# The order in which attention takes its sixteen (group, chunk) pairs: two groups mixed, or one group after the other

## The reference

```python
q = _rope(proj(Wq, bq), e); k = _rope(proj(Wk, bk), e); v = proj(Wv, bv)
att = jnp.einsum('bhqd,bhkd->bhqk', q, k) / scale
att = jnp.where(causal[None, None], att, -jnp.inf)
att = jax.nn.softmax(att, axis=-1)
y = jnp.einsum('bhqk,bhkd->bqhd', att, v)   # then the output projection
...
x = x + 0.5 * ffn(layernorm(x))     # ffn: attention, router, top 2 of 8 experts
x = x + attn(layernorm(x))
x = x + 0.5 * ffn(layernorm(x))
```

## Time and profile before

| | us |
|---|---|
| median of 3 runs | 1795.04 |
| lowest and highest | 1793.52, 1797.59 |
| profiled execution | 1790.89 |
| its span, first to last instruction | 1789.1 |

### The profile page before, as it was taken

The page is one execution under the profiler, slowest core; times in us unless marked ns, Lnnn a source line. Parts: engine busy times, 40 slices in busy tenths (PEclk is TensorE's granted clock), DMA queues, the critical chain, the costliest instruction groups (busy, mean ns, idle before and its releaser), DMA issues. The chain is left out here.

```text
span 1789.1 us, 31832 instructions
## 1 busy us (share of the span) xinstructions
PE 1629.0 (91%) x11268; PEld 751.0 (42%) x11268; DVE 1387.4 (78%) x3068; ACT 1143.6 (64%) x2427; POOL 413.1 (23%) x485
## 2 busy tenths in 40 slices
PE   5899999999949957999999999889999999996795
PEld 3333333334239933433333333344333333332795
DVE  6899978899256657999798996289997989963665
ACT  6365776777846734655777767546557677676565
POOL 5112111001017724103102010151031020100574
PEclk9999999999969979999999999899999999998898
DMA  5300023110011235100202000151002020000113
GB/s 161 101 23 2 1 55 101 40 41 2 2 38 48 49 103 162 42 1 2 54 2 55 3 2 1 58 161 42 2 2 55 2 55 3 2 2 32 36 49 95
DMA packets 58702, 75.48 MB, mean 42 GB/s; under 512 B 12303, under 2 KB 49492, under 8 KB 57424
## 3 DMA queue, kind: packets, MB, share of 16 engines
q1 hardware_dynamic: 52163, 61.86, 12.8%
q0 software_dynamic: 4992, 9.40, 2.1%
q10 hardware_dynamic: 1389, 2.17, 0.3%
HBM read 52.86 MB, written 21.46 MB: 42 GB/s over the span
## 5 line engine op out<-in xcount | busy, mean ns | idle before, releaser
L848 ACT ACTIVATE probs<-ps 128x512 f32<-128x512 f32 (+3 forms) x1920 | 879.0, 544 | 418.7 <-PE ps L993 417.1
L688 DVE TENSOR_REDUCE mpart<-ps 128x1 f32<-128x512 f32 (+3 forms) x1680 | 1014.0, 666 | 111.4 <-PE ps L937 54.5
L937 PE MATMUL ps<-ka,qa 96*128 96x512 bf16 (+3 forms) x1920 | 642.7, 352 | 11.9 <-DMA ka<-ksplit 7.1
L993 PE MATMUL ps<-qa,ka 96*128 96x512 bf16 (+3 forms) x1920 | 601.4, 349 | 8.9 <-DMA qa<-guard 8.2
L1006 PE MATMUL ps<-probs,vv 128*9 128x512 f32 (+3 forms) x3840 | 441.3, 531 | 13.5 <-ACT probs L848 7.7
L795 POOL TENSOR_SCALAR_AFFINE_SELECT probs<-probs 128x512 f32<-128x512 f32 x192 | 121.6, 634 | 1159.2 <-ACT probs L848 1158.9
L937 PEld LDWEIGHTS ps<-ka,qa 96*128 96x128 bf16 x1920 | 186.9, 98 | 438.0 <-DVE mpart L688 317.5
L993 PEld LDWEIGHTS ps<-qa,ka 96*128 96x128 bf16 x1920 | 180.8, 98 | 186.5 <-ACT probs L848 68.7
L940 PE MATMUL ps<-mask_rows,identb 128*128 128x128 bf16 x768 | 152.2, 223 | 0.0
L1006 PEld LDWEIGHTS ps<-probs,vv 128*9 128x9 f32 x3840 | 57.8, 88 | 162.2 <-ACT probs L848 119.5
L1281 ACT ACTIVATE probs<-wgu,ln2s 128x896 f32 x78 | 81.1, 1042 | 56.0 <-DVE eti L1152 28.1
(11 more groups left out here) (196 smaller groups left out, 1231.4 us busy)
## 6 DMA issues: line engine op xcount, KB each, us to landing
qa<-qsplit SPq DMA_DIRECT2D x72, 96.0 KB
ka<-ksplit SPq DMA_DIRECT2D x72, 96.0 KB
qa<-qsplit SPq DMA_DIRECT2D x18, 384.0 KB
ka<-ksplit SPq DMA_DIRECT2D x18, 384.0 KB
probs<-rope SPq DMA_DIRECT2D x12, 512.0 KB, 5.8
qsplit<-arena SPq DMA_DIRECT2D x6, 384.0 KB, 3.5
ksplit<-arena SPq DMA_DIRECT2D x6, 384.0 KB, 2.7
tokens<-arena SPq DMA_DIRECT2D x2, 1040.0 KB, 3.8
```

The lines of the kernel that those rows point to most:

```text
L688: dve.tensor_reduce(mpart[:, j % MD, h0:h0 + some, qt, kc], ps[:, bank, 0:some * w].rearrange("p (h w) -> p h w", h=some), axis=AX.X, op=A ...
L848: act.activation(probs[:, s % 2, h, 0:n], ps[:, u % SB, 0:n], ACT.Exp, scale=SCALE).then_inc(probs_ready, 1)
L937: ins = pe.matmul(dst, qa[0:KROWS, b, h0 + k, tile * 128:(tile + 1) * 128], ka[0:KROWS, b, h0 + k, kc * CH:kc * CH + n], start=True, stop= ...
L993: pe.matmul(dst, ka[0:KROWS, b, h, kt * 128:(kt + 1) * 128], qa[0:KROWS, b, h, c * CH + q0:(c + 1) * CH], start=True, stop=True).then_inc( ...
```

## The change

The list is written without the mixing. Before, the first eight turns are (0,0) (0,1) (1,0) (1,1) (0,2) (0,3) (1,2) (1,3). Now they are (0,0) (0,1) (0,2) (0,3) (1,0) (1,1) (1,2) (1,3). Groups 2 and 3 keep their order. Everything that is derived from the list (the schedule, the numbers that the waits compare with, the place of the reloads) follows. Lines of the changed kernel are two less than those of before.

```diff
-    chunks = [(0, 0), (0, 1), (1, 0), (1, 1), (0, 2), (0, 3), (1, 2), (1, 3)]
-    for g in range(2, NG):
-        chunks += [(g, c) for c in range(NC)]
+    chunks = [(g, c) for g in range(NG) for c in range(NC)]
     left = {g: max(j for j, ch in enumerate(chunks) if ch[0] == g) + 1 for g in range(NG)}
```

## The result

| | before | after |
|---|---|---|
| median of 20 runs, us | 1793.44 | 1807.04 |
| lowest and highest | 1788.22, 1801.20 | 1795.52, 1811.55 |
| ratio, with its interval | | 1.0075 [1.0063, 1.0086] |
| profiled execution, us | 1790.89 | 1807.12 |
| mean granted clock in it | 0.963 | 0.959 |

The changed kernel is 0.75% slower, by 13.6 us. The forecast was 1804.9 us, +9.9. The page after, as the earlier trace rows: PE's busy time is 9.7 us longer, the other engines' busy times have moved by less than 3 us, and the span is 16.2 us longer.

What follows compares the result with a forecast made beforehand. The prediction took PE's work list to bound the kernel; per layer, 1.6 us for the reload and 1.7 for the gaps, times three, gave +9.9 us on 1795.0, so 1804.9 us. The 8-in-10 range was 1798.0 to 1811.5.

Steps and rivals of the forecast that it cites:

- What bounds the kernel: Attention turns: PE's work list sets their length, since one more fill costs 0.25 us, near PE's 0.22, not DVE's 0.60.
- The reload of group 0: Moved from (1,2) to (1,0), its 3.50 us zeroing delays masks that PE's values need: +1.6 us a layer.
- The gaps: ACT's idle times before (0,1), (0,2), (0,3): the second grows from 8.33 to 10.9 us, net +1.7 us a layer.
- The rest of the schedule at nothing: A fuller (1,2), with fills taken out of (2,3) and (3,2): 0, bounds -1 and +1 us a layer.
- The loads of chunks 2 and 3 at nothing: Group 0's chunks 2 and 3 are used earlier in the order, but their loads arrive in time: no cost.
- The clock at nothing: TensorE's granted clock stays 1.00 in turns that wait, as in (2,0) before: nothing added.
- Rival 1: DVE is the bound, so filling its idle time in (1,2) makes the kernel faster: 1781.5 us on the runs; chance 0.08.
- Rival 2: No change: waiting fills cover the zeroing and only four dummies a layer remain, +2.6 us, 1797.7 us; chance 0.11.
- Rival 3: Guard-row copies for (1,2) queue behind the reload's loads and come late: 15 us more, 1819.9 us; chance 0.04.

Runs made afterwards that it cites:

- x_r0_at_11: The changed kernel with the reload of group 0 one turn later, at the start of (1,1); ratio 1.0025 to the kernel before.
- x_r0_at_12: The changed kernel with the reload of group 0 at the start of (1,2), as before the change; ratio 1.0036 to the kernel before.
- x_quarters: The changed kernel with the zeroing cut into four parts, one behind each mask of (1,0) and (2,0); ratio 1.0011 to the kernel before.
- y_before_r1_later: The kernel before with its second reload, for group 3, at (2,1) instead of (2,0); ratio 0.9996 to the kernel before.
- y_best: The kernel before with its second reload at the third step of (2,1) and the planner's guard-row allowance cut from 5500 to 4200; ratio 1.0057.
- z_zero_twice: The changed kernel with the zeroing of guard rows done twice, one after the other, at both reloads; ratio 1.0248 to the kernel before.

## Why the prediction was right, and where it wasn't

**What bounds the kernel.** Right. The comparison of turns said that DVE's idle time is free, and x_r0_at_11 against x_r0_at_12 shows it directly: 2.9 or 8.7 us of idleness, the same time. The Trainium skill's rule (Perfetto Trace Analysis, Identifying the Most-Contended Engine) would have given 1781.5; here it names the wrong engine, with DVE at 77% and weight loads at 42%.

**The reload of group 0.** Right in place and size: 1.6 forecast, 1.65 measured by moving it alone.

**The gaps.** Right in kind. The second gap is 10.84 for a forecast of 10.9, 2.5 us more than it was. The net, what is left of the 3.0 us a layer without the reload's 1.65, is 1.3 or 1.4 and not 1.7, so what the moved fills give back comes out at 1.2 and not 0.9.

**The rest of the schedule at nothing.** Right: 273.7 us from (1,2) to the end in both orders, though single turns moved by up to 2.9 us, (1,2) up, (2,3) and (3,2) down, as said.

**The loads of chunks 2 and 3 at nothing.** Right: between 1207 and 1342 us, from within (0,0), where the first fills of (0,2) now stand, to the end of (0,3), PE waits for no load, and the turns' lengths are the same in all three layers.

**The clock at nothing.** This step failed. The forecast reasoned from the earlier trace rows, where (2,0) has the same wait and a clock of 1.00. One kind of turn, three times in one execution, was too little for it. With two such turns a layer the clock fell in five of the twelve that were profiled, for 1.4 to 1.6 us each (with what it costs in the next turn), and with dummies ahead of the wait in none of six. That is 4.5 and 3.1 us in the two executions. Nor is the wait in (2,0) the same one: it went from 1.63 to 1.75 us, and in all three layers of the kernel before a moment at which the clock can change fell into it. The difference between the kernels was forecast at 9.9 us and measured at 13.6: 4.5 were missing for the clock, and the other terms were 1.0 too large. That the time itself came out only 2.1 us too low is in part luck, because the median it started from, 1795.04, was 1.6 above the one of 20 runs. TensorE: Matmul & The Clock Gate of the Trainium skill ("Part 1") speaks of idle gaps longer than these as the cause of a lowered clock; the rows above show it after waits of 1.63 and 1.75 us too.

**The range.** 1798.0 to 1811.5 doesn't come out of its own words. One microsecond a layer less in each of two terms gives 1798.9, and half of the way to the two upper ends gives 1809.1; the measured 1807.04 lies inside these too. No allowance in it was made for the clock.

**Rival 1** fell with x_r0_at_12. **Rival 2** fell with (1,0), 10.13 us and not 8.9. **Rival 3** was real and didn't decide: in the changed kernel SP sends the second copy for (1,2) at 1365.93, 23.8 us after the start of (1,0) (forecast 23.6), and nothing waits; SP's timeline, as the earlier trace rows:

```profile
1352.60 0.32 SPq L439 DMA_DIRECT2D guard<-arena  x1
1365.93 0.71 SPq L441 DMA_DIRECT2D qa<-guard  x1
```

In x_quarters it goes out 27.2 us after that start, while (1,2) is due 1.65 us sooner. That takes 5.0 us of margin in all, and PE waits 1.06, so the margin was about 4 us, as the prediction had put it. Its 2.5 us for the landing of the second copy stood on no row; in x_quarters PE starts 2.4 us after that copy is sent.

## What to carry to other kernels

Look behind every long instruction of a helper engine for short ones that the critical engine waits for: 3.5 us of zeroing cost nothing where a mask was four steps away, 1.65 us where one was queued behind it, and 1.0 us where it only met a cast on another engine. A stall on PE has a second price beside its length, the clock behind it, and one profile with a clock of 1.00 doesn't prove that price to be zero; adding stalls, or filling one with dummies, shows it, and so does laying the waits beside the moments at which the clock changed. Before a transfer is moved later, work out the margin of the small copies that queue behind it.

## What the runs showed of the hardware

A DVE cast from SBUF to SBUF (16x128, f32 to bf16) of 0.21 us took 1.66 us (y_before_r1_later) and 3.03 us (y_best) when it met POOL's zeroing, in every layer, and ended less than 0.1 us behind it. The reductions that met a zeroing kept their lengths, and so did a cast from PSUM (0.27 us) and a subtraction with a PSUM operand (0.28), so it isn't DVE as a whole that stood still. The Trainium skill (SBUF — State Buffer, SBUF: two separate sides) says that DVE and GpSimd share a pair of ports that one instruction holds until it ends, and that a DVE operation which needs the shared pair then waits. The trace agrees: the cast ends right behind the zeroing.

The clock fell after PE's waits of 1.63 to 1.75 us in five turns of 21 (five of the twelve in the changed kernel), after 2.66 us in two layers of three (y_best), and after 5.19 or 5.31 us in six of six (z_zero_twice). It changed only at evenly spaced moments. Of the ten short waits that ended before the next of these moments four were followed by the lower clock, of the eleven that such a moment fell into one was.

The same kernel took 1793 us on one chip and 1848 to 1853 on others, with attention turns equal to some hundredths of a microsecond. For the changed kernel the profiled executions differ by 56.1 us in their spans, and 31.7 of it lies between the attention turns of the first and the second layer, 24.9 behind the last turn of the third. These are the phases of the two layers with experts; why they take longer there isn't known.
